# Local attention: queries and keys pass the two shared PSUM banks by halves, with a signal for each half

## What is computed

```python
def _L0_ffn_ref(x, wqkv, q_scale, k_scale, wo, ...):   # 8 heads of 64, window 64, 2 x 1024 tokens
    for l in range(2):
        h = shift_token(x)
        q, k, v = split(h @ wqkv[l], 3)                 # 512 columns each
        q = l2norm(q) * q_scale[l]                      # per head
        k = l2norm(k) * k_scale[l]
        q = q * cos * scale + rotate_half(q) * sin * scale
        k = k * cos / scale + rotate_half(k) * sin / scale
        o = local_attention(q, k, v)                    # each block of 64 sees itself and the one before
        x = x + o @ wo[l]
        x = x + gated_gelu_feed_forward(layernorm(shift_token(x)))
    return x

x = x + 0.5 * _L0_ffn_ref(layernorm(x), ...)
x = x + linear_attention(layernorm(x))
x = x + 0.5 * _L0_ffn_ref(layernorm(x), ...)
...                                                     # layers 1 to 3: not touched
```

## Time and profile before

| | us |
|---|---|
| median of 3 runs | 2387.69 |
| lowest and highest run | 2384.38, 2388.55 |
| profiled execution | 2391.73 |
| its span, first to last instruction | 2389.9 |
| PE busy | 2117.3 (89%) |
| DVE busy | 1547.4 (65%) |
| ACT busy | 1193.1 (50%) |
| POOL busy | 518.1 (22%) |

### The profile page before, as it was taken

How to read it: one execution, slowest core, us unless ns; L and a number is a source line. 1 busy time by engine, 2 the same in 40 slices (tenths; PEclk the granted TensorE clock), 3 DMA queues, 4 the chain that set the end, 5 groups by cost and what they waited for, 6 DMA issues and landing times. The chain is left out here.

```text
span 2389.9 us, 40305 instructions
## 1 busy us (share of the span) xinstructions
PE 2117.3 (89%) x15567; PEld 1165.4 (49%) x15567; DVE 1547.4 (65%) x2995; ACT 1193.1 (50%) x2102; POOL 518.1 (22%) x836
## 2 busy tenths in 40 slices
PE   5988998796999898899699999989957957999999
PEld 3665665474666566445212222234535745455454
DVE  7986896656886897401888888641087778057650
ACT  4774773254774675321267877742133643242421
POOL 4331330213331331000544343100013110000000
PEclk8999999897999999999789999999988977999999
DMA  4000000001000000000211111000000110000000
GB/s 143 4 6 3 4 4 5 6 3 51 4 4 5 1 7 6 27 0 1 90 49 43 44 52 35 19 10 0 0 5 3 41 51 10 0 1 1 1 9 9
DMA packets 47681, 45.16 MB, mean 19 GB/s; under 512 B 33026, under 2 KB 37826, under 8 KB 46722
## 3 DMA queue, kind: packets, MB, share of 16 engines
q1 hardware_dynamic: 38386, 34.90, 4.8%
q0 software_dynamic: 9104, 7.68, 1.2%
HBM read 34.18 MB, written 4.46 MB: 16 GB/s over the span
## 5 line engine op out<-in xcount | busy, mean ns | idle before, releaser
L2306 DVE TENSOR_REDUCE fa_top<-psum 128x1 f32<-128x1024 f32 x256 | 299.4, 1217 | 48.7 <-PE psum L2205 48.7
L2282 ACT ACTIVATE fa_prob<-psum 128x512 f32<-128x512 f32 x512 | 275.2, 597 | 98.4 <-PE psum L2247 98.1
L758 POOL TENSOR_TENSOR turn_a<-turn_a,turn_b 128x1024 f32<-128x1024 f32 x64 | 151.1, 2361 | 286.2 <-DVE turn_b L976 286.2
L2173 POOL DMA_DIRECT2D area_a<-fa_parts_dram x240 | 133.1, 557 | 141.7 <-issue 141.4
L2247 PE MATMUL psum<-fa_stack_q,fa_stack_k 74*128 74x512 bf16 x512 | 159.2, 394 | 4.5 <-ACT fa_prob L2282 2.0
L775 PE MATMUL psum<-area_a,zt 128*128 128x512 f32 x256 | 135.7, 655 | 24.3 <-ACT k_t L907 14.3
L549 DVE TENSOR_TENSOR scaled<-psum,area_b 128x512 f32<-128x512 f32 x8 | 5.5, 691 | 213.1 <-PE psum L518 213.1
L2260 PE MATMUL psum<-fa_prob,fa_pair_v 128*32 128x512 f32 x1024 | 139.7, 618 | 0.0
L3597 PE MATMUL psum<-hidden_a,area_b 128*128 128x512 f32 x256 | 112.5, 592 | 0.0
L2203 PE MATMUL psum<-fa_stack_k,fa_stack_q 64*128 64x512 bf16 x256 | 88.1, 410 | 27.1 <-DVE fa_top L2306 19.9
L3597 PE MATMUL psum<-hidden_b,area_b 128*128 128x512 f32 x256 | 111.5, 592 | 0.0
(11 more groups left out here) (400 smaller groups left out, 4651.0 us busy)
## 6 DMA issues: line engine op xcount, KB each, us to landing
area_b<-in_L_ffn SPq DMA_DIRECT2D x2, 2888.0 KB, 9.4
fa_stack_q<-fa_parts_dram SPq DMA_DIRECT2D x144, 32.0 KB
fa_stack_k<-fa_parts_dram SPq DMA_DIRECT2D x144, 32.0 KB
area_a<-fa_parts_dram POOLq DMA_DIRECT2D x120, 32.0 KB, 2.3
fa_parts_dram<-fa_prob SPq DMA_DIRECT2D x12, 256.0 KB, 2.5
area_a<-in_L_ffn SPq DMA_DIRECT2D x1, 2482.0 KB, 18.2
moved_halves<-y SPq DMA_DIRECT2D x16, 127.0 KB
area_a<-fa_parts_dram POOLq DMA_DIRECT2D x120, 16.0 KB, 2.3
```

The costliest lines, as they stand in the source:

```text
L758: nc.gpsimd.tensor_tensor(turn_a[:], turn_a[:], turn_b[:], ALU.add).then_inc(rotary_sums.handle, 1)
L2173: pool.dma_start(to[at:at + D, :, :], parts_dram[b, which, pair[which]].rearrange("(h d) t -> d h t", d=D)[:, 2 * q:2 * q + 2, tokens]).th ...
L2282: nc.scalar.activation(prob[:, (2 * s + j) % RING, half * CHUNK:(half + 1) * CHUNK], slot_bank("scores", n), ACT.Exp, scale=float(D) ** -0 ...
L2306: nc.vector.tensor_reduce(top[:, g % 2, j, t:t + 1], psum[:, 2 * j:2 * j + 2, :].rearrange("p a n -> p (a n)"), AX.X, ALU.max, negate=True ...
```

## The change

Each hand-over of q and k gets one signal for each half instead of one for both, so the five semaphores `qk_made`, `squared`, `products`, `qk_turned` and `qk_taken` count two to a tile. `pe_qk` waits and signals for each half; `act_square` becomes two activations; the first rotary product becomes two instructions, and the order on DVE is then q direct, q crossed, k direct, k crossed; `pe_turn_qk` waits and signals for each half; `act_take_qk` copies q after the first signal and k after the second. Waits elsewhere (`pool_rotary_sum`, `pe_scores`, `dve_square_sum`, `dve_norm_qk`, `pe_turn_tokens`) ask for the second half's count.

```diff
             g = l * TILES + n
-            pool.wait_ge(*products.at(g + 1))
+            pool.wait_ge(*products.at(2 * g + 2))
...
-            if n >= 3:
-                pe.wait_ge(*qk_taken.at(g - 1))
-            elif n:
-                pe.wait_ge(*products.at(g))
-            elif l:
-                pe.wait_ge(*qk_taken.at(g))
             if l and n % PER_CHUNK == 0:
                 pe.wait_ge(*next_taken.at(n // PER_CHUNK + 1))
             for s in range(2):
-                last = nc.tensor.matmul(qk_banks[:, s, :], zt[:, 64 + n * P:64 + (n + 1) * P], wq[:, s * LA_INNER:(s + 1) * LA_INNER],
-                                        start=True, stop=True)
-            last.then_inc(qk_made.handle, 1)
+                if n >= 3:
+                    pe.wait_ge(*qk_taken.at(2 * (g - 2) + s + 1))
+                elif n:
+                    pe.wait_ge(*products.at(2 * (g - 1) + s + 1))
+                elif l:
+                    pe.wait_ge(*qk_taken.at(2 * (g - 1) + s + 1))
+                nc.tensor.matmul(qk_banks[:, s, :], zt[:, 64 + n * P:64 + (n + 1) * P], wq[:, s * LA_INNER:(s + 1) * LA_INNER],
+                                 start=True, stop=True).then_inc(qk_made.handle, 1)
...
             pe.wait_ge(*rotated.at(g + 1))
-            if n:
-                pe.wait_ge(*products.at(l * TILES + min(n + 2, TILES)))
-            elif l:
+            if l and n == 0:
                 pe.wait_ge(*gated.at(l * UPS))
             for s in range(2):
+                if n:
+                    pe.wait_ge(*products.at(2 * (l * TILES + min(n + 1, TILES - 1)) + s + 1))
                 for k in range(K):
                     last = nc.tensor.transpose(turn_banks(n)[:, s, k * P:(k + 1) * P],
                                                qk[:, s * H + 2 * k:s * H + 2 * k + 2, :], core.ident[:])
-            last.then_inc(qk_turned.handle, 1)
+                last.then_inc(qk_turned.handle, 1)
...
-            act.wait_ge(*qk_made.at(g + 1))
-            nc.scalar.activation(squares[:], qk_banks.rearrange("p b (h d) -> p (b h) d", d=D), ACT.Square).then_inc(squared.handle, 1)
+            for s in range(2):
+                act.wait_ge(*qk_made.at(2 * g + s + 1))
+                nc.scalar.activation(squares[:, s * H:(s + 1) * H, :], qk_banks[:, s, :].rearrange("p (h d) -> p h d", d=D),
+                                     ACT.Square).then_inc(squared.handle, 1)
...
-            act.wait_ge(*qk_turned.at(g + 1))
-            nc.scalar.copy(q_t[:], turn_banks(n)[:, 0, :].rearrange("p (k n) -> p k n", k=K))
+            act.wait_ge(*qk_turned.at(2 * g + 1))
+            nc.scalar.copy(q_t[:], turn_banks(n)[:, 0, :].rearrange("p (k n) -> p k n", k=K)).then_inc(qk_taken.handle, 1)
             act.wait_ge(*window_moved.at(g + 1))
+            act.wait_ge(*qk_turned.at(2 * g + 2))
             nc.scalar.copy(k_t[:, :, 0:3:2, :], turn_banks(n)[:, 1, :].rearrange("p (k a n) -> p k a n", k=K, a=2)).then_inc(qk_taken.handle, 1)
...
-            dve.wait_ge(*squared.at(g + 1))
             t = n % SEQ_TILES
-            nc.vector.tensor_tensor(turn_a[:].rearrange("p (s h) d -> p s h d", s=2), qk_banks.rearrange("p s (h d) -> p s h d", d=D),
-                                    direct[:, :, t:t + 1, :].to_broadcast([P, 2, H, D]), ALU.mult)
             for s in range(2):
+                dve.wait_ge(*squared.at(2 * g + s + 1))
+                nc.vector.tensor_tensor(turn_a[:, s * H:(s + 1) * H, :], qk_banks[:, s, :].rearrange("p (h d) -> p h d", d=D),
+                                        direct[:, s, t:t + 1, :].to_broadcast([P, H, D]), ALU.mult)
                 partner = qk_banks[:, s, :].rearrange("p (h a d) -> p h a d", h=H, a=2)[:, :, ::-1, :]
                 last = nc.vector.tensor_tensor(turn_b[:, s * H:(s + 1) * H, :].rearrange("p h (a d) -> p h a d", a=2), partner,
                                                cross[:, s, t:t + 1, :].to_broadcast([P, H, D]).rearrange("p h (a d) -> p h a d", a=2),
                                                ALU.mult)
-            last.then_inc(products.handle, 1)
+                last.then_inc(products.handle, 1)
```

More of the change, by code:

```diff
@@ L809, in pe_scores @@
                 pe.wait_ge(*shifted_s.at(g))
-            pe.wait_ge(*qk_taken.at(g + 1))
+            pe.wait_ge(*qk_taken.at(2 * g + 2))
             for s in range(2):
@@ L956, in dve_square_sum @@
                 dve.wait_ge(*norms.at(g - 1))
-            dve.wait_ge(*squared.at(g + 1))
+            dve.wait_ge(*squared.at(2 * g + 2))
             nc.vector.tensor_reduce(square_sum[:, p], squares[:], AX.X, ALU.add).then_inc(summed_squares.handle, 1)
@@ L985, in dve_norm_qk @@
             if g:
-                dve.wait_ge(*qk_turned.at(g))
+                dve.wait_ge(*qk_turned.at(2 * g))
             dve.wait_ge(*norms.at(g + 1))
@@ L1084, in pe_turn_tokens @@
             if c < 2:
-                pe.wait_ge(*qk_taken.at((l + 1) * TILES))
+                pe.wait_ge(*qk_taken.at(2 * (l + 1) * TILES))
             elif c == 2:
@@ L1473, in l0_ffn @@
         first.close()
+        for tally in (qk_made, squared, products, qk_turned, qk_taken):
+            tally.done += 2 * TILES
         first_cleared.done += BATCH
```

## The result

| | before | after |
|---|---|---|
| median, us | 2387.5 | 2361.8 |
| lowest and highest run | 2384.4, 2397.4 | 2361.2, 2363.6 |
| profiled execution: span | 2389.9 | 2360.3 |
| up to the end of the second local stage, "the touched part": start of its last residual step (L1157, after: L1159) | 969.9 | 945.4 |
| the rest of the span, no line of it touched | 1420.0 | 1415.0 |

The ratio is 0.9889, with a 95% interval of 0.9872 to 0.9907: 25.8 us faster by the medians. The forecast was 2368 in a range of 2357 to 2382. The touched part is not pure either: between the local attention loops it holds feed-forward and linear attention code that is the same in all kernels.

A forecast was written before the change was run, and what follows sets the result against it. Two loops without slack, squares and PE, set the 8.92 us turn; the two-turn loop would then set 8.64. Settled turns 11.2, first turns 6.2 and 0.8, layer ends 1.6: 19.8 off 2387.7 gives 2368, range 2357 to 2382.

The forecast's parts named there:

- The settled turn: One steady interval of the local attention loop, 40 in all; forecast to shrink from 8.92 to 8.64 us, saving 11.2.
- Loop 3: Two-turn wait loop through products, transposes, copies, logarithm and norm; 17.61 us before, forecast 17.27, or 8.64 a turn, setting the turn.
- Loop 2: PE's wait loop through projection, scores, transposes and both copies; 8.92 us without slack, forecast at most 8.62.
- loop 1: The squares loop, from rotary products through the exponential to the next squares; 8.92 us without slack, forecast 8.54.
- The cost of the products by halves: Splitting the first rotary product on DVE: forecast to add about 0.05 us a turn, bounds 0 and 0.14.
- Transposes and copies: The q copy needs only the first four of eight transposes: forecast 0.44 us sooner; the k copy's second wait adds 0.05.
- Projection: The q half of the q and k projection on PE waits for the q copy alone: forecast to start 0.30 us sooner.
- First turns and layer ends: Gains outside the settled loop: 6.2 us in first layers, 0.8 in second layers, 1.6 at layer ends.
- A: Rival: ScalarE keeps the norm late, so loop 3 stays at 8.86 us a turn; 2378 us, chance 0.16.
- B: Rival: more slack than thought, PE's weight load spared, loop 1 sets the turn at 8.54; 2364 us, chance 0.15.
- C: Rival: DVE is the true bound and its waits are only replaced; only first turns gain, 2384 us or above, chance 0.08.
- D: Rival: added waits inside projection and transposes make PE the bound, 9.2 us a turn; slower, 2396 us, chance 0.06.

The follow-up runs named there:

- all but the squares: The changed kernel, but with the squares as one activation and the first rotary product as one instruction, as before; 2386.9 us, ratio 0.9981.
- squares and products only: The kernel before, with only squares and rotary products by halves; projections, transposes and copies keep one wait and signal for both; 2383.7 us, ratio 0.9974.
- the whole first product: The changed kernel, but the first rotary product is one instruction for both banks, waiting for both halved squares; 2385.0 us, ratio 0.9984.
- late q copy: The changed kernel, but the q copy waits until the transposes of both halves are done, as before; 2377.0 us, ratio 0.9942.
- POOL halves with the order kept: The changed kernel with POOL's rotary sum also by halves, ScalarE's order staying copies first, then norm; 2347.4 us, ratio 0.9827.

## Why the prediction was right, point by point

**The settled turn: right in its mechanism, too small by a fifth.** 8.64 was forecast and 8.59 measured: 0.05 of the difference between the saving of 0.36 and my 0.28 is there. The other 0.03 is that I set 8.64 against a turn of 8.92 and not against the mean of 8.95. By the four layers: 3.6, 3.4, 3.5 and 3.7, together 14.2 us, against 11.2.

**Loop 3 was the right one.** With the rows above: L975 to L1002 5.04, to L918 1.32, to L834 1.11, L834 to L799 4.95, to L906 0.64, to L909 0.49, to L889 0.48, to L991 1.88, to L975 1.26. Sum 17.17, or 8.59 a turn; I had 17.27. Three terms were mis-sized. L916 to L835, 1.24, I took for a latency; it held PE's own work on L775, which ended only then, and is 1.11 now, as it is in the kernel with all but the squares, where PE stands idle for 0.28 before L834. The second wait of the k copy, put at 0.05, costs 0.01 (0.49 against 0.48). L834 to L799 is 0.06 longer, and why is not shown. Delaying the q copy gave loop 3 its 0.43 back and the turn 0.22.

**Loop 2 had no slack, loop 1 had 0.06.** PE's loop alone holds 8.94 (squares and products only), the squares loop alone 8.86 (all but squares). I had called both tight; the 0.53 of L948 to L881 hid a short wait.

**The cost of the products by halves.** L975 to L758 is 2.62 (103.59 to 106.21) against 2.56 before: 0.06 a turn, forecast 0.05. The Trainium skill's section on the TRN2 errata in "VectorE: DVE Perf Modes" would have made it 0.125; start to start, the rows show half of that. The half square takes 0.599, forecast 0.59.

**Transposes and copies.** L799 to L906 fell from 1.08 to 0.64, as forecast. **Projection.** The early start of the q half is hidden in the settled loop and needn't be there; the forecast had given it 0.30 in loop 2, which the early copies give alone. The logarithm was to come 0.3 sooner behind L1000 (it was 0.57 behind it); it comes 0.08 sooner in one turn and 0.25 in the other.

**First turns and layer ends.** 24.5 less 14.2 leaves 10.3 us, forecast 8.6. In the first layer the sixth rotary sum starts 3.4 sooner (66.72 to 63.35), forecast 3.1: 1.7 of it are there at the first sum (forecast 1.6). In these first turns the parts don't add up either, and the early q copy is not needed: that sum starts 0.4 sooner with squares and products only, 1.0 with all but the squares, 1.5 with the whole first product, and 3.6 with the late q copy. The other 6.9 us are read from one profile on either side, and no experiment takes them apart. By stretches they don't match: from the last sum of a first layer to the sixth of the second, 0.7 in the first stage and 3.0 in the second, where 0.8 was forecast for each. Unchanged code lies between, at a granted clock of 1.00 before and 0.97 after in the one, and 0.97 and 1.00 in the other. So it is partly luck that the sum comes so near.

**The rivals.** A (8.86 a turn) is what the kernel with the late q copy does, at 8.81: it is the right loop, and the change avoids it. B (8.54) named the squares loop as the next one; it sums to 8.50, the shorter of the alternating turns. C is out: DVE idles less and the turn shrinks. D is out: no idle time shows inside L775 or L799 in the settled turn, over the whole run that before L799 is 28.1 us against 27.2, and with one wait fewer in the projection nothing changes. D's own sum took the 0.30 off twice: PE's 8.62 and three waits of 0.30 are 9.52 and not 9.2, so D would have been slower still.

## What to carry to other kernels

When several loops through different engines have the same length, no single wait has a price: sum each loop from the timeline, start to start, and expect little from a change until all of them are shorter. In this kernel the square by halves paid only with its consumer split too; and a start that follows another "without idle" may still hide a wait of a few hundredths, so a step's length should be checked against a place where nothing else could have held it.

## What the runs showed that I had not expected

The part of the kernel that no edit touches, from the end of the second local stage to the end, took between 1411.5 and 1424.6 us in the ten profiled executions. Two of them, in the view of one stretch (length, busy time of PE, PEld, DVE, ACT and POOL, then the granted clock in parts of full speed, DMA share and GB/s), first POOL halves with the order kept and then the whole first product:

```profile
934.00:2345.50 1411.50, 1259.84 (x6831) 581.97 (x6831) 799.06 (x1587) 625.32 (x1086) 235.28 (x380) 0.95 0.08 21
```

```profile
967.80:2392.40 1424.60, 1277.09 (x6831) 588.80 (x6831) 799.33 (x1587) 625.53 (x1086) 235.27 (x380) 0.93 0.07 21
```

DVE, ACT and POOL are busy for the same time to 0.3 us, PE for 17 us more in the longer one, at a granted clock of 0.93 against 0.95 (levels of 1.2 and 2.4 GHz, and more of the stretch at the lower). I tell this as seen together, not as shown cause: no run changed the clock by itself. It is part of why the span of two profiles differs by 29.6 us where the medians differ by 25.8, and why the touched part, not the span, was compared.

The same goes on inside the touched part. Between the loops of the two layers the granted clock was 1.00 in the first stage (158 to 212 us) and 0.97 in the second (708 to 763 us) before, 0.97 and 1.00 with the change, and 0.94 in both with all but the squares. From the last rotary sum of the first layer to the first of the second, the kernel before took 56.0 and 56.7 us and all but the squares 57.9 in both, which outweighs what its settled turns gain.
